# Second FFN: the first left-over block routed ahead of the shared expert, and 71 expert tiles a call instead of 72

## What is computed

```python
x = x + 0.5 * ffn(layernorm(x))
x = x + mixer_block(layernorm(x))
x = x + 0.5 * ffn(layernorm(x))

def ffn(x):      # 8 experts, the 2 best for each token, hidden size 256
    shared = (silu(x @ sw1) * (x @ sw2)) @ sw3
    probs = softmax(x @ rw + rb)
    w, idx = top_k(probs, 2)
    w = w / sum(w)
    gates = sum(w[..., None] * one_hot(idx, 8))
    h = silu(x @ ew1[e]) * (x @ ew2[e])        # for every expert e
    return shared + sum over e of (h @ ew3[e]) * gates[e]
```

## Time and profile before

| | us |
|---|---|
| median of 3 runs | 791.8 |
| lowest, highest | 791.72, 792.77 |
| profiled execution | 793.16 |
| its span | 791.1 |
| TensorE matmuls busy | 649.5 (82%) |
| VectorE busy | 548.8 (69%) |
| ScalarE busy | 424.9 (54%) |
| GpSimd busy | 519.5 (66%) |

### The profile page before, as it was taken

How to read it: one execution, slowest core, us unless ns; L and a number is a source line. 1 busy time by engine, 2 the same in 40 slices (tenths; PEclk the granted TensorE clock), 3 DMA queues, 4 the chain that set the end, 5 groups by cost and what they waited for, 6 DMA issues and landing times.

```text
span 791.1 us, 13711 instructions
## 1 busy us (share of the span) xinstructions
PE 649.5 (82%) x3768; PEld 478.4 (60%) x3768; DVE 548.8 (69%) x1706; ACT 424.9 (54%) x745; POOL 519.5 (66%) x656
## 2 busy tenths in 40 slices
PE   3478979999907298989999997999978979999950
PEld 2245558888802155657576665667635557889840
DVE  5666756656549669897999999899735635566637
ACT  1122224554407999898999998643213214445525
POOL 3777765666646676887898869676754442666660
PEclk9988989999957588999999999979989998999995
DMA  9511223333142000000000000000010113333218
GB/s 264 161 45 51 78 69 85 88 88 92 57 143 77 0 1 1 0 2 1 1 2 1 1 15 15 14 15 22 21 34 25 58 35 87 86 94 89 79 30 316
DMA packets 49368, 46.34 MB, mean 59 GB/s; under 512 B 8456, under 2 KB 42861, under 8 KB 49296
## 3 DMA queue, kind: packets, MB, share of 16 engines
q1 hardware_dynamic: 40592, 28.54, 12.9%
q0 software_dynamic: 8704, 16.93, 6.6%
HBM read 25.30 MB, written 21.19 MB: 59 GB/s over the span
## 4 chain that ended last, share of the span: by engine, by line
PE 30%; POOL 25%; issue 16%; DVE 12%; DMA 8%; ACT 8%; POOLq 1%; SPq 0%; DVEq 0%; ACTq 0%
POOL xs L710 11%; POOL ys L726 11%; DMA xs<-rows,pos 6%; PE ps_tr L1662 4%; PE ps_go L1662 3%; PE ps_tr L2064 2%; PE ps_go L2051 1%; PE ps_go L1833 1%; PE ps_tr L1850 1%; PE ps_go L1837 1%; PE ps_b L1884 1%; POOL rstd L700 1%; PE ps_go L1883 1%; PE ps_a L2038 1%; PE ps_a L2039 1%
## 5 line engine op out<-in xcount | busy, mean ns | idle before, releaser
L726 POOL DMA_INDIRECT ys<-arena,dest x144 | 140.8, 978 | 88.9 <-issue 64.7
L710 POOL DMA_INDIRECT xs<-rows,pos x128 | 127.0, 993 | 76.2 <-DMA xs<-rows,pos 32.3
L1006 ACT ACTIVATE silu_a<-ps_a 128x512 f32<-128x512 f32 x32 | 19.1, 597 | 62.0 <-PE ps_a L2002 62.0
L2064 PE MATMUL ps_tr<-w_down_e,arena 128*128 x384 | 50.7, 275 | 0.0
L1521 DVE TENSOR_TENSOR hid<-silu_a,ps_a 128x512 f32<-128x512 f32 x36 | 24.8, 688 | 34.8 <-ACT silu_a L1026 34.8
L1521 DVE TENSOR_TENSOR hid<-silu_a,ps_b 128x512 f32<-128x512 f32 x36 | 24.8, 688 | 34.3 <-ACT silu_a L1026 34.3
L2064 PEld LDWEIGHTS ps_tr<-w_down_e,arena 128*128 128x128 f32 x384 | 46.7, 192 | 0.0
L1035 ACT ACTIVATE arena<-ps_go 128x512 f32<-128x512 f32 x72 | 42.6, 592 | 2.0 <-PE ps_go L2051 2.0
L1488 DVE TENSOR_TENSOR hid<-silu_a,ps_b 128x512 f32<-128x512 f32 x32 | 21.9, 687 | 31.2 <-PE ps_b L2004 29.3
L2051 PE MATMUL ps_go<-ident,hid 128*128 128x128 f32 x288 | 43.2, 272 | 0.2
L1026 ACT ACTIVATE silu_a<-ps_a 128x512 f32<-128x512 f32 x36 | 21.5, 597 | 38.4 <-PE ps_a L2040 38.4
(11 more groups left out here) (368 smaller groups left out, 2042.3 us busy)
## 6 DMA issues: line engine op xcount, KB each, us to landing
arena<-xs SPq DMA_DIRECT2D x144, 65.0 KB, 1.9
rows<-ys SPq DMA_DIRECT2D x8, 512.0 KB, 3.8
arena<-ys SPq DMA_DIRECT2D x8, 512.0 KB, 7.1
ys<-arena,dest POOLq DMA_INDIRECT x144
x<-in_L_attn_x SPq DMA_DIRECT2D x8, 256.0 KB, 4.5
arena<-in_L_ffn_ew SPq DMA_DIRECT2D x4, 512.0 KB, 7.0
xs<-rows,pos POOLq DMA_INDIRECT x128
out<-x SPq DMA_DIRECT2D x8, 256.0 KB, 4.8
```

Of the source, the lines that this page charges most:

```text
L710: pool.indirect_dma_start(xs, bass.IndirectOffsetOnAxis(pos[:, n, i:i + 1], 0), rows[:, n * TT + i % TT, :], None).then_inc(scattered, 16)
L726: pool.indirect_dma_start(ys, bass.IndirectOffsetOnAxis(dest[:, i:i + 1], 0), y_out[:, p % YRING, j, :], None, bounds_check=2 * TOK - 1, o ...
L2064: r = pe.matmul(ps_answers(p)[:, j * P:(j + 1) * P], hid_t[:, p % 2, at:at + P], w_down_e[:, bass.ds(which[2 * p + j], 1), k, :].rearrange ...
```

## The change

**Routing of the left-over blocks.** Block 5 is routed before round 0: its transposes go to the buffer `ps_k`, its logits to `ps_r`, and its choice is VectorE's first work in the second FFN. Block 6 takes the place that block 5 had, and block 7 that of block 6. In `dve_ffn_again` the choice of the next block now comes ahead of the normalisation of block 7, where it came behind. The tile table follows in round 2 instead of round 3.

**Tiles.** LIVE = 71 tiles are loaded, worked on and stored. The last pair has one tile; its operations are half as wide, and the waits count accordingly.

```diff
+LIVE = NT - 1
+def tiles_of(p):
+    return range(2 * p, min(2 * p + 2, LIVE))
...
         def act_ffn_again(act):
+            act_route_xt(act, EARLY, ps_k)
             act_xt(act, NB)
             act_xt(act, NB + 1)
             for n in range(NB):
                 act_silu(act, NB + n, 0)
-                if EARLY + n < NB:
-                    act_route_xt(act, EARLY + n, ps_t)
+                if EARLY + n + 1 < NB:
+                    act_route_xt(act, EARLY + n + 1, ps_t)
...
         def dve_ffn_again(dve, own):
             dve.wait_ge(mixer_done, NB)
+            dve_route(dve, own, NB + EARLY)
             for n in range(NB + 1):
+                late = EARLY + n + 1
                 if n < NB:
                     dve_hid(dve, NB + n, 0)
-                if 1 <= n <= NB - EARLY:
-                    dve_places(dve, own, NB + EARLY + n - 1)
+                if late - 1 < NB:
+                    dve_places(dve, own, NB + late - 1)
                 if n < NB:
                     dve_hid(dve, NB + n, 1)
+                if n:
+                    dve_shared(dve, NB + n - 1)
+                if late < NB:
+                    dve_route(dve, own, NB + late)
                 if n == 0:
                     dve_norm(dve, NB + NB - 1)
-                if n:
-                    dve_shared(dve, NB + n - 1)
-                if n < NB - EARLY:
-                    dve_route(dve, own, NB + EARLY + n)
-                if n == NB - EARLY:
+                if late == NB:
                     dve_tiles(dve, own, 1)
...
             pe.wait_ge(mixer_done, NB)
             pe.wait_ge(rank_read, NB + EARLY)
+            pe_route_xt(pe, EARLY, ps_k)
             pe_xt(pe, NB)
+            pe_route_logits(pe, EARLY, ps_r)
             pe_xt(pe, NB + 1)
             for n in range(NB + 1):
-                late = EARLY + n
+                late = EARLY + n + 1
                 if n < NB:
                     pe_up(pe, NB + n, 0)
                 if late < NB:
                     pe.wait_ge(xt_ready, NB + n + 2)
                     pe_route_xt(pe, late, ps_t)
-                if 0 <= n - 1 < NB - EARLY:
+                if late - 1 < NB:
                     pe.wait_ge(rank_read, NB + late - 1)
                     pe_rank(pe, NB + late - 1)
...
             pool.wait_ge(answer_ready, pair + 1)
-            for j in range(2):
-                i = 2 * p + j
+            for j, i in enumerate(tiles_of(p)):
                 pool.indirect_dma_start(ys, bass.IndirectOffsetOnAxis(dest[:, i:i + 1], 0),
```

More of the change, by code:

```diff
@@ L54, with in_ring @@
 ARENA = 9219
+def tiles_of(p):
+    return range(2 * p, min(2 * p + 2, LIVE))
+def in_ring(r, ring, of=1):
+    return sum(i // of % ring == r for i in range(LIVE))
 class Steps:
@@ L455, in _ @@
                 sp.wait_ge(b_ps_ready, 2 * NB * (call + 1))
-                for i in range(NT):
+                for i in range(LIVE):
                     if i and i % GROUP == 0:
@@ L463, in _ @@
                 for r in range(YRING):
-                    sp.wait_ge(y_stored[r], 32 * (NPAIR // YRING) * (call + 1))
+                    sp.wait_ge(y_stored[r], 16 * in_ring(r, YRING, 2) * (call + 1))
                 ring = BACK[call]
@@ L1034, in act_hid_t @@
                 act.wait_ge(y_ps_ready, pair - 1)
-            act.activation(hid_t[:, p % 2, :], ps_d, ACT.Copy).then_inc(ht_ready, 1)
+            width = len(tiles_of(p)) * HID
+            act.activation(hid_t[:, p % 2, 0:width], ps_d[:, 0:width], ACT.Copy).then_inc(ht_ready, 1)
         def act_finish(act):
@@ L2021, in pe_tiles_t @@
                 pe.wait_ge(answer_ready, pair - 4)
-            for j in range(2):
-                i = 2 * p + j
-                pe.wait_ge(tile_in[i % XIN], 16 * ((call * NT + i) // XIN + 1))
+            for j, i in enumerate(tiles_of(p)):
+                pe.wait_ge(tile_in[i % XIN], 16 * (call * in_ring(i % XIN, XIN) + i // XIN + 1))
                 r = pe.transpose(ps_tiles(p)[:, j * P:(j + 1) * P], x_tiles[:, i % XIN, 0:P], ident[:, :])
@@ L2032, in pe_up_e @@
             after(pe, hid_e_done, pair - 1)
-            for j in range(2):
-                hi = up_hi[:, bass.ds(which[2 * p + j], 1), :].rearrange("p a h -> p (a h)")
-                lo = up_lo[:, bass.ds(which[2 * p + j], 1), :].rearrange("p a h -> p (a h)")
+            for j, i in enumerate(tiles_of(p)):
+                hi = up_hi[:, bass.ds(which[i], 1), :].rearrange("p a h -> p (a h)")
+                lo = up_lo[:, bass.ds(which[i], 1), :].rearrange("p a h -> p (a h)")
                 target = ps_pair[p % 2][:, j, :]
@@ L2047, in pe_hid_t @@
             after(pe, ht_ready, pair)
-            for j in range(2):
+            for j in range(len(tiles_of(p))):
                 for k in range(2):
@@ L2064, in pe_down_e @@
                     r = pe.matmul(ps_answers(p)[:, j * P:(j + 1) * P], hid_t[:, p % 2, at:at + P],
-                                  w_down_e[:, bass.ds(which[2 * p + j], 1), k, :].rearrange("p a d -> p (a d)"),
+                                  w_down_e[:, bass.ds(which[i], 1), k, :].rearrange("p a d -> p (a d)"),
                                   start=(k == 0), stop=(k == 1))
```

25 lines of the change are left out of this document (13 added, 12 removed).

## The result

The changed kernel takes 786.34 us (median of 12 executions, 784.03 to 792.01), the kernel before 792.59 beside it (12 executions, 791.64 to 793.52). The ratio is 0.9928, 95% interval 0.9911 to 0.9945. Forecast were 784.7 us and 782.4 to 787.2. All ratios here leave out executions over 1.5% slower than the fastest one of their kernel; the medians do not.

The account below looks back on a forecast made before the run. The prediction took a chain of stages as the bound, with GpSimd's scatters and landings binding the second FFN and its answers ending each expert stage. 791.8 - 4.20 - 1.45 - 1.45 gave 784.7 us, range 782.4 to 787.2.

Parts of the forecast that it names:

- Part 1: Second FFN: routing block 5 first lets its first scatter start at 599.27 instead of 603.47, -4.20 us.
- the pair of 596.21 lands at about 598.5: Second FFN: block 4's last scatter pair lands about when GpSimd finishes rstd (598.58), so block 5's first scatter can follow.
- the 12 pairs keep their pace: Second FFN: the scatter pairs of blocks 5 to 7 stay 4.03 us apart; no change, allowing ±1.0 us.
- TensorE's slack: Second FFN: TensorE leaves the shared expert near 645.0, 3.3 us less idle, with 4.5 us to spare before the tiles.
- The rival that TensorE becomes the bound: Second FFN: new waits let the clock fall and the shared expert runs at half speed, up to 820 us; chance 0.02.
- that of late routing: Second FFN: `pos` of block 5 comes after 599, losing up to 4.2 us, 785.5 to 788.9 us; chance 0.09.
- The rule on shared ports: Second FFN: VectorE's normalisation and GpSimd's scatter could block each other, costing up to 1.12 us; the trace row said 0 to 0.13.
- Part 2: Expert stages of both calls: 71 tiles leave GpSimd one answer fewer at the end, -1.45 us in each call.
- Part 3: Start of the experts: TensorE's clock around the first tile could cost 1.5 us or gain 1.8; taken as 0.
- The rival of the mixer: Mixer: its chain swallows the first call's 1.45 us by another phase of the clock, 786.2 us; chance 0.04.
- The sum: Whole kernel: -4.20 - 1.45 - 1.45 = -7.1 us, from 791.8 to 784.7 us.

Follow-up runs that it names:

- e1: The changed kernel run again unaltered on chip B, a slower chip: 843.13 us, ratio 0.9985 to the kernel before.
- e3: The kernel before with only the second FFN's new order, still 72 tiles, on chip B: 841.54 us, ratio 0.9963 to the kernel before.
- f1: The changed kernel run again unaltered on chip A, a fast chip: 789.42 us, ratio 0.9959 to the kernel before.
- f2: The kernel before with only the second FFN's new order, still 72 tiles, on chip A: 790.49 us, ratio 0.9955 to the kernel before.
- f4: The changed kernel with call 1's pad stores issued only after all scatters have landed, on chip A: 793.33 us, ratio 0.9996 to the kernel before.
- e2: The changed kernel with the second FFN's old order, so only 71 tiles are new, on chip B: 846.02 us, ratio 1.0010 to the kernel before.

## Why the prediction was right, and where not

- **Part 1, the wait for `pos`**: right as to the mechanism. `pos` of block 5 was written from 10.2 us after the mixer's last addition instead of 16.7 (forecast, as the earliest start of the scatter, 10.4 on this scale), before GpSimd was free, and in the profiles after, e1 and e3 the first scatter came 3.3 to 4.5 us earlier. In f1, f2 and f4 it came 2.4 to 2.6 earlier, because the step "the pair of 596.21 lands at about 598.5" failed: that landing now took 4.05 to 4.31 us.
- **Part 1, "the 12 pairs keep their pace"**: this step was mis-sized. It stood at 0 ± 1.0 and measured +2.2 in the first profile (+2.5 and +2.1 in f1 and f2). Part of it is that the one profile of before had the best pace of all eight, which one trace can't tell; by the means of the eight the pace cost 0.7 (47.6 against 46.9) and the start was 3.1 earlier, not 4.2. Part may be that the wait removed had been cover, with two instruction loads under it; that is argued from coincidence. The forecast looked for cover only among the kernel's own steps (pads, table loads). With both steps, Part 1 was −2.1 in the first profile and about −2.5 over all profiles, not −4.2.
- **TensorE's slack**: TensorE was forecast to leave the shared expert 5.06 + 3.3 us earlier than before (639.9 on the scale of after), and measured 641.09, so 2.1 earlier instead of 3.3; the gap was 5.45 where 4.5 was forecast. The rival that TensorE becomes the bound, and that of late routing, are out.
- **The rule on shared ports** ("SBUF — State Buffer", "Who interferes with whom", of the Trainium skill): L1420 ran from 595.48 for 1.10 us beside the scatter of 595.33, which took 0.96, and L1404 had taken 1.12 before. Neither lost anything.
- **Part 2**: right in the stages, −1.49 and −1.56 against −1.45 each, by the mechanism named (6.44 us from pair 32's last answer to the last one). That the 2.9 us arrive in the whole time is not shown: the one usable run of the tiles alone (e2, chip B) was 0.1% slower than before.
- **Part 3, the clock on the ramp**: 0 was right for the first profile (rise between 650.5 and 651.5, 4.5 us after the first tile, as before). In f1 the rise came 6 us after it. The Trainium skill ("TensorE: Matmul & The Clock Gate", "Part 1: The HAM clock gate") has the gate's window run free of the program, and such a change from run to run agrees with that, though f1's gap was also longer.
- **The rival of the mixer** ("the first call's gain doesn't pass through", 0.04) was held too small. Over the profiles the mixer moves by up to 7.4 us with its granted clock (2.0 us for each 0.01), in both directions. That call 0's gain is swallowed there is not shown, as its clock was no lower with 71 tiles than with 72. On chips A and B the changed kernel was granted 0.005 and 0.008 less than the one before over the whole execution; on chip A this would be 1.6 to 1.8 us of the gain, by the estimate above.
- **The sum**: −7.1 forecast, −6.25 measured there, inside the range. By stages it would have been −5.7 without the mixer (0.3 + 1.5 + 2.1 + 1.6 + 0.2). Part 1 fell short by half and the range was wide enough for that. That the result lies inside it is in part luck: on chip A, with less clock granted, the same comparison gave −3.95, where the range's upper end stood for −4.6.

## What to carry to other kernels

A wait in a latency-bound chain of DMAs may also cover what the profile's groups don't list: before pricing its removal, look up the instruction queues in that stretch and ask which landing they may meet next. The pace of such a chain, read from one trace, can be the best of several. Where landings set the pace, let a second transfer be in flight rather than start the chain earlier: here, on a chip of the fast kind, that was worth 9.1 us and the reordering about 2 to 3. And for a kernel whose time goes with the granted clock, give the clock of each execution beside its time; 3.5 us for each 0.01 is half of what was to be measured here. Where a profile says "remote", look in the kernel's text for the semaphore that is waited for before calling the engine ready.

## What was not expected of the hardware

- An indirect scatter lands in 2.3 us, and in 2.7 to 4.5 beside plain stores from SyncE or with an instruction load inside (in time; the cause is not shown, and three loads did nothing).
- Chips differ by 6 to 7% on this kernel (793 against 844 and 847 us), nearly all of it in stretches where scatters follow each other at 1.27 us; there TensorE's signals come up to 12.9 us late, and VectorE and ScalarE wait for them up to 13.9 us. Two pairs in flight gain 1.7% on one kind of chip. On the other they gain 0.6% by the ratio (seven executions) and 0.1% by the medians, and their stage takes 71.2 and 74.3 us where kernels that wait pair by pair take 64.5 to 69.8.
- The mean granted clock of equal executions on one chip ranged from 0.902 to 0.922, and the time with it by 8 us.
- The mixer, with the same instructions in all 14 profiles, took from 358.9 to 366.3 us as its mean granted clock went from 0.909 to 0.877.
